# First chunk of a macaron block: affinities and choice in halves, and a new order of ScalarE's first work

## The reference

```python
def ffn(x, centroids, expert_biases, Ws_up, Ws_down, W_up, W_down):
    shared = silu(xf @ Ws_up) @ Ws_down
    aff = xf @ centroids.T                        # 64 experts
    _, idx = top_k(aff + expert_biases, 8)
    w = sigmoid(take_along_axis(aff, idx, axis=1))
    w = w / (sum(w, axis=-1, keepdims=True) + 1e-08)
    cw = zeros((T, E)).at[arange(T)[:, None], idx].add(w)
    h = silu(einsum('td,edf->etf', xf, W_up))     # F = 64
    y = einsum('etf,efd->etd', h, W_down)
    return shared + einsum('etd,te->td', y, cw)

def attn(x, Wq, Wk, Wv):
    q, k, v = x @ Wq.T, x @ Wk.T, x @ Wv.T
    return softmax(q @ k.T) / sqrt(128) @ v       # all 2048 keys

x = x + 0.5 * ffn(layernorm(x), ...)
x = x + attn(layernorm(x), Wq, Wk, Wv)
x = x + 0.5 * ffn(layernorm(x), ...)
```

## Time and profile before

| what | value |
|---|---|
| profiled execution, its own time | 541.02 us |
| its span, first to last instruction | 539.2 us |
| TensorE busy | 532.0 us (99%) |
| VectorE busy | 408.5 us (76%) |
| ScalarE busy | 407.0 us (75%) |
| GpSimd busy | 273.7 us (51%) |
| mean granted clock of TensorE | 1.000 |
| HBM traffic over the span | 133 GB/s |

### The profile page before, as it was taken

The page is one execution under the profiler, slowest core; times in us unless marked ns, Lnnn a source line. Parts: engine busy times, 40 slices in busy tenths (PEclk is TensorE's granted clock), DMA queues, the critical chain, the costliest instruction groups (busy, mean ns, idle before and its releaser), DMA issues.

```text
span 539.2 us, 8716 instructions
## 1 busy us (share of the span) xinstructions
PE 532.0 (99%) x2710; PEld 437.2 (81%) x2710; DVE 408.5 (76%) x933; ACT 407.0 (75%) x815; POOL 273.7 (51%) x242
## 2 busy tenths in 40 slices
PE   8999999999999999999999999999999999999997
PEld 6677887887888888799999999878887888788886
DVE  5998689877966677867777889779678767965664
ACT  6898778877877775866666657778779777877773
POOL 3689757775776764000000000267676676766663
PEclk9999999999999999999999999999999999999999
DMA  8675555554555550000000000155565565556662
GB/s 264 194 220 200 189 182 167 179 197 150 172 187 193 190 160 1 2 1 0 1 2 1 2 1 0 50 193 171 166 195 169 168 202 169 182 157 204 202 193 84
DMA packets 44270, 72.25 MB, mean 134 GB/s; under 512 B 8864, under 2 KB 9632, under 8 KB 44224
## 3 DMA queue, kind: packets, MB, share of 16 engines
q1 hardware_dynamic: 43568, 71.17, 42.0%
q10 hardware_dynamic: 592, 0.39, 0.3%
q0 software_dynamic: 64, 0.13, 0.1%
HBM read 69.57 MB, written 2.10 MB: 133 GB/s over the span
## 4 chain that ended last, share of the span: by engine, by line
PE 93%; DVE 3%; ACT 2%; issue 1%; POOL 0%; DVEq 0%; POOLq 0%
PE lrow L1174 13%; PE lrow L1175 13%; PE lrow L1176 13%; PE bank L1216 11%; PE bank L1218 10%; PE bank L1217 10%; PE bank L1279 5%; PE bank L1501 3%; PE bank L1503 3%; PE bank L1502 3%; PE bank L1393 1%; PE bank L1286 1%; PE bank L1175 1%; PE bank L1176 1%; PE bank L1174 1%
## 5 line engine op out<-in xcount | busy, mean ns | idle before, releaser
L295 POOL TENSOR_TENSOR gpart_lo<-gated,gpart_hi 128x512 fp32r<-128x512 f32 x174 | 223.7, 1295 | 162.9 <-ACT gpart_hi L462 161.3
L451 ACT ACTIVATE lrow<-lrow 128x512 f32<-128x512 f32 (+1 forms) x245 | 143.9, 587 | 62.4 <-PE lrow L1176 61.9
L718 DVE TENSOR_TENSOR gated<-lrow,wide 128x512 f32<-128x512 f32 x170 | 116.1, 683 | 56.3 <-ACT lrow L451 53.6
L462 ACT CAST gpart_hi<-gated 128x512 fp32r<-128x512 f32 x174 | 106.7, 613 | 5.9 <-DVE gated L718 5.3
L1216 PE MATMUL bank<-gpart_lo,wdn_hi 128*128 128x512 f32 x246 | 97.7, 397 | 0.0
L1218 PE MATMUL bank<-gpart_hi,wdn_hi 128*128 128x512 f32 x246 | 97.7, 397 | 0.0
L1217 PE MATMUL bank<-gpart_hi,wdn_lo 128*128 128x512 f32 x246 | 97.0, 394 | 0.0
L718 DVE TENSOR_TENSOR lrow<-lrow,wide 128x512 f32<-128x512 f32 x74 | 51.4, 695 | 26.9 <-ACT lrow L451 26.9
L1092 DVE TENSOR_TENSOR pT_lo<-bank,pT_hi 128x512 fp32r<-128x512 f32 x64 | 43.6, 683 | 21.7 <-ACT pT_hi L650 21.7
L295 DVE TENSOR_TENSOR gpart_lo<-lrow,gpart_hi 128x512 fp32r<-128x512 f32 (+1 forms) x83 | 56.5, 681 | 1.6 <-ACT gpart_hi L462 1.3
L650 ACT CAST pT_hi<-bank 128x512 fp32r<-128x512 f32 x64 | 38.1, 595 | 24.1 <-PE bank L1279 23.9
(11 more groups left out here) (281 smaller groups left out, 978.2 us busy)
## 6 DMA issues: line engine op xcount, KB each, us to landing
wide<-gates_dram SPq DMA_DIRECT2D x488, 128.0 KB, 3.0
raw<-in_w_up SPq DMA_DIRECT2D x8, 256.0 KB, 5.5
raw<-in_w_down SPq DMA_DIRECT2D x8, 256.0 KB, 5.7
gates_dram<-gates SPq DMA_DIRECT2D x8, 128.0 KB, 2.3
x<-in_x SPq DMA_DIRECT2D x3, 256.0 KB, 3.9
out_dram<-x SPq DMA_DIRECT2D x3, 256.0 KB, 3.1
x<-in_x SPq DMA_DIRECT2D x1, 128.0 KB, 2.3
x<-in_x ACTq DMA_DIRECT2D x1, 128.0 KB, 2.5
```

Source lines behind the costliest of these rows:

```text
L295: return eng.tensor_tensor(gpart[1][0:m, U % NGP, :], gated_at(U)[0:m, :], gpart[0][0:m, U % NGP, :].bitcast(F32), ALU.subtract)
L451: nc.scalar.activation(dst[0:m, :], hid[U % NH][0:m, :], ACT.Silu).then_inc(s_silu, 1)
L462: nc.scalar.copy(gpart[0][0:m, U % NGP, :], gated_at(U)[0:m, :]).then_inc(s_ghi, 1)
L718: nc.vector.tensor_tensor(gated_at(U), a, b, ALU.mult).then_inc(s_gated, 1)
```

## The change

Six edits, all for the first chunk. (1) The affinities of tiles 2 and 3 go to another PSUM bank than those of tiles 0 and 1, each half has its own semaphore, and VectorE adds the bias and takes the maxima half by half; the sigmoid is two activations too. (2) GpSimd makes the cast of the small weights and waits, before its second `piece_lo`, for the experts' weights. (3) ScalarE makes the selector and the copy of the shared down weights before the first piece, and the second piece before the sigmoids. (4) ScalarE copies the turned weights before the third piece; the copy of the gates, and the pieces from the fourth on, come behind later units. (5) The transfer of the value weights moves from ScalarE's queue, and those of the query and key weights from GpSimd's queue, to SyncE at unit 31. (6) The semaphore for the shared down weights is split from that of the value weights.

```diff
@@ SyncE, chunk loop
                     if n == 0 and u % 2 == 1 and FIRST + (u - NB) // 2 < 2 * WP:
                         load_piece(FIRST + (u - NB) // 2)
+                    if n == 0 and u == 31:
+                        sp.dma_start(raws[:, E + F:LOADED], wv_d).then_inc(s_value, 16)
+                        for i, src in enumerate((wq_d, wk_d)):
+                            sp.dma_start(raw_qk[:, i * D:(i + 1) * D], src).then_inc(s_qk, 16)
@@ GpSimd
-            for i, src in enumerate((wq_d, wk_d)):
-                nc.gpsimd.dma_start(raw_qk[:, i * D:(i + 1) * D], src).then_inc(s_qk, 16)
             ...
+            pool.wait_ge(s_small, 16 * 2)
+            nc.gpsimd.tensor_copy(small[0][:, 0:E + F], raws[:, 0:E + F]).then_inc(s_wh0, 1)
             ...
                     if n == 0:
-                        for k in range(PRE):
+                        piece_lo(0)
+                        pool.wait_ge(p_cw, 1)
+                        for k in range(1, PRE):
                             piece_lo(k)
@@ ScalarE
+            def first_sil(h):
+                act.wait_ge(f_bias, h + 1)
+                nc.scalar.activation(sil[:, h * GT:(h + 1) * GT, :].rearrange("p t e -> p (t e)"),
+                                     (bank[0], mp)[h][:, 0:GT * E], ACT.Sigmoid).then_inc((f_sil, p_sil)[h], 1)
-            act.dma_start(raws[:, E + F:LOADED], wv_d).then_inc(s_value, 16)
-            act.wait_ge(s_small, 16 * 2)
-            nc.scalar.copy(small[0][:, 0:E + F], raws[:, 0:E + F]).then_inc(s_wh, 1)
                             first_hi(0)
                             first_hi(1)
-                            piece_hi(0)
-                            act.wait_ge(s_value, 16 * 3)
-                            nc.scalar.copy(wsdn[0][:, :], rawd[:, :]).then_inc(s_wh, 1)
                             act.wait_ge(s_spread, 1)
                             make_sel()
-                            act.wait_ge(f_bias, 1)
-                            nc.scalar.activation(flat(sil), bank[0][:, 0:TPC * E], ACT.Sigmoid).then_inc(p_sil, 1)
+                            act.wait_ge(s_sdn, 16 * 2)
+                            nc.scalar.copy(wsdn[0][:, :], rawd[:, :]).then_inc(s_wh, 1)
+                            piece_hi(0)
+                            piece_hi(1)
+                            first_sil(0)
+                            first_sil(1)
                             nc.scalar.activation(eps[:, 3:4], eps[:, 0:1], ACT.Silu)
-                            piece_hi(1)
                             silu_unit(0, n)
                             silu_unit(1, n)
                             hi_unit(0, n)
                             silu_unit(2, n)
+                            act.wait_ge(p_cwT, 1)
+                            nc.scalar.copy(cwT[:, :], mp[:, :]).then_inc(p_cwr, 1)
                             piece_hi(2)
+                            silu_unit(3, n)
+                            hi_unit(1, n)
                             pro_cwT(n)
-                            silu_unit(3, n)
-                    for u in range(7 if n == NCH else min(c, 1), UNITS):
+                            hi_unit(2, n)
+                            silu_unit(4, n)
+                            piece_hi(PRE)
+                            hi_unit(3, n)
+                            piece_hi(PRE + 1)
+                            silu_unit(5, n)
+                            hi_unit(4, n)
+                            piece_hi(PRE + 2)
+                    for u in range((6, 7)[f] if c == 0 else 1, UNITS):
@@ VectorE, first_top
-                dve.wait_ge(p_aff, 1)
-                nc.vector.tensor_tensor(b[:, :, :], bank[0][:, 0:TPC * E].rearrange("p (t e) -> p t e", e=E),
-                                        bc(bias[:, :]), ALU.add).then_inc(f_bias, 1)
-                dve.wait_ge(f_bias, 1)
-                for i in range(TPC):
-                    ins = nc.vector.max(top[:, i, :], b[:, i, :])
+                for h in range(2):
+                    some = slice(h * GT, (h + 1) * GT)
+                    dve.wait_ge((f_aff, p_aff)[h], 1)
+                    nc.vector.tensor_tensor(b[:, some, :], (bank[0], mp)[h][:, 0:GT * E].rearrange("p (t e) -> p t e", e=E),
+                                            bias[:, :].unsqueeze(1).to_broadcast([P, GT, E]), ALU.add).then_inc(f_bias, 1)
+                    dve.wait_ge(f_bias, h + 1)
+                    for i in range(h * GT, (h + 1) * GT):
+                        ins = nc.vector.max(top[:, i, :], b[:, i, :])
                 ins.then_inc(p_max, 1)
@@ TensorE, first_aff
-                    ins = product(bank[0][:, i * E:(i + 1) * E], [a[:, 0, i * P:(i + 1) * P] for a in xnT[0]], cen)
-                ins.then_inc(p_aff, 1)
+                    at = i % GT * E
+                    ins = product((bank[0], mp)[i // GT][:, at:at + E], [a[:, 0, i * P:(i + 1) * P] for a in xnT[0]], cen)
+                    if i % GT == GT - 1:
+                        ins.then_inc((f_aff, p_aff)[i // GT], 1)
```

More of the change, by code:

```diff
@@ L157, in macaron_kernel @@
         s_x0b = sem("x_in0_second_half")
-        s_small, s_value, s_qk, s_bias = sem("small_in"), sem("value_in"), sem("qk_in"), sem("bias_in")
+        s_small, s_sdn, s_value, s_qk, s_bias = (
+            sem("small_in"), sem("shared_down_in"), sem("value_in"), sem("qk_in"), sem("bias_in"))
         s_eps, s_zero = sem("eps_made"), sem("cw_zeroed")
@@ L162, in macaron_kernel @@
         s_pad = sem("wsdn_pad_zeroed")
-        f_xT, f_hi, f_lo, f_bias = (sem("first_" + n) for n in ("xT", "hi", "lo", "biased"))
+        f_xT, f_hi, f_lo, f_aff, f_bias, f_sil = (sem("first_" + n) for n in ("xT", "hi", "lo", "aff", "biased", "sigmoid"))
         s_raw = [sem(f"raw_in{i}") for i in range(NR)]
@@ L168, in macaron_kernel @@
         s_id, s_spread = sem("ident_made"), sem("spread_made")
-        s_wh, s_wl = sem("small_hi_made"), sem("small_lo_made")
+        s_wh0, s_wh, s_wl = sem("first_small_hi_made"), sem("small_hi_made"), sem("small_lo_made")
         s_whi = sem("weight_piece_hi")
@@ L491, in pro_cwT @@
                 act.wait_ge(p_cwT, n + 1)
-                if n % NCH == 0:
+                if n == NCH:
                     nc.scalar.copy(cwT[:, :], mp[:, :]).then_inc(p_cwr, 1)
@@ L585, in _ @@
                             silu_unit(2, n)
+                            act.wait_ge(p_cwT, 1)
+                            nc.scalar.copy(cwT[:, :], mp[:, :]).then_inc(p_cwr, 1)
                             piece_hi(2)
+                            silu_unit(3, n)
+                            hi_unit(1, n)
                             pro_cwT(n)
-                            silu_unit(3, n)
-                    for u in range(7 if n == NCH else min(c, 1), UNITS):
+                            hi_unit(2, n)
[7 more added lines that the diff above has]
+                    for u in range((6, 7)[f] if c == 0 else 1, UNITS):
                         if c or u >= LEADS[f]:
                             silu_unit(u, n)
-                        if c or u > 1 - f:
-                            hi_unit(*before(u, n))
+                        hi_unit(*before(u, n))
                         if n == 0 and u % 2 == 0 and PRE + u // 2 < 2 * WP:
@@ L620, in _ @@
                         if n == 1 and u == 4:
+                            act.wait_ge(s_value, 16)
                             nc.scalar.copy(small[0][:, E + F:LOADED], raws[:, E + F:LOADED]).then_inc(s_wh, 1)
@@ L983, in small_lo @@
                             def small_lo(k, parts, whole, lo, hi):
[L984 removed]
+                                dve.wait_ge(s_wh if k else s_wh0, max(k, 1))
                                 nc.vector.tensor_tensor(parts[1][:, lo:hi], whole[:, lo:hi], parts[0][:, lo:hi].bitcast(F32),
```

5 lines of the change are left out of this document (2 added, 3 removed).

## The result

The changed kernel takes 542.42 us (median of 22 runs, 541.56 to 543.27), the kernel before 541.18 on the same chip (22 runs). The ratio is 1.0018, 95% interval 1.0012 to 1.0025: 1.0 us slower (0.6 to 1.4), less than the 0.5% that the prediction set as its bound for a change. The medians differ by 1.24. The ratio is smaller: it agrees with that of the means, 542.35 and 541.36, and one long execution, 543.68, lifts the mean of the kernel before (such executions are the subject of the last experiment). The profiled execution has a span of 540.5, 1.3 above the 539.2 of before. The forecast was 1.4 us slower, at 542.9.

The account below looks back on a forecast made before the run. TensorE's matmul stream and its holes bound the kernel (93% of the span). VectorE's wait for GpSimd's root (1.3) plus unit 13's gates (0.1) gave +1.4 on 541.5: 542.9 us, range 540.9 to 544.8; the 0.2 gained earlier did not count.

Parts of the forecast that it names:

- Start: Before the affinities: the first transpose stays at 5.96 and everything up to the affinity products keeps its place within 0.05 us.
- Halves: VectorE's bias and maxima by halves: choice multiply moves from 11.33 to about 10.89, 0.44 us sooner (bounds 0.3 and 0.52).
- First piece 0.93 later: ScalarE's first piece at 8.32 moves the first expert product to 10.58; TensorE is free at 13.56, net gain 0.2 us.
- GpSimd's wait costs 0: GpSimd's second subtraction waits for the experts' weights (13.1); only subtractions needed behind 20 us follow, so cost 0.
- The root: GpSimd's second-chunk root ends at 22.8; VectorE's normalisation moves from 21.55 to 22.83: 1.3 us lost (bounds 0 and 2.3).
- Unit 13's gates: Late gates' copy: unit 13's second half lands at 34.7, its user comes at 34.45; 0.1 us lost (bounds 0 and 0.5).
- Loads at unit 31 cost nothing: SyncE issues gates of units 31 to 33 1.8 us later; unit 31's, 0.8 late, covered by 7 us before down matmuls.
- Rival B: Faster: GpSimd's root ends before VectorE needs it at 21.4, gaining 0.44 and 0.2, to 540.9 us; chance 0.14.
- Rival C: No change: the stall is given back as later first-chunk holes shrink by 1.1 us; +0.3, 541.8 us; chance 0.17.
- Rival D: Much slower: late gates count, 1.3 plus 0.25 at unit 13 and 0.8 at unit 31; +2.4, 543.9 us; chance 0.14.
- sign of being wrong: Second chunk: the forecast is wrong if GpSimd's root ends before 21.5 or the transposes come before 25.2.
- the other case: Clock rival: TensorE runs at half rate for 4 us behind the new hole, 2 us more, 544.9 us; chance 0.03.

Follow-up runs that it names:

- the last experiment: The run also called cast only: kernel before, with just the cast of the small weights moved from ScalarE to GpSimd; 540.96 us, ratio 0.9993.
- cast only: Kernel before, with just the cast of the small weights moved from ScalarE to GpSimd; 540.96 us, ratio 0.9993 to the kernel before.
- loads only: Kernel before, with just the loads of the value, query and key weights moved to SyncE at unit 31; 541.13 us, ratio 0.9996.
- halves only: Kernel before, with just the affinities, bias, maxima and sigmoids in halves; 540.75 us, ratio 0.9989.
- piece first: The head only kernel, with the first weight piece again ahead of the selector and the shared weights' copy; 540.34 us, ratio 0.9984 to the kernel before.
- one warm-up fewer: The head only kernel, with one warm-up matmul instead of two ahead of the expert weights' transposes; 540.29 us, ratio 0.9984 to the kernel before.
- head only: The change, with ScalarE's order of third piece, turned weights, gates' copy and later pieces put back as before; 540.46 us, ratio 0.9982 to the kernel before.
- Root first: The change, with GpSimd's reciprocal root for the second chunk ahead of the fourth piece's low part; 542.30 us, ratio 1.0016 to the kernel before.
- both: The change, with GpSimd's root ahead of the fourth piece and the gates' copy directly behind the turned weights' copy; 540.51 us, ratio 0.9984.
- gates early: The change, with the gates' copy directly behind the copy of the turned weights; 541.63 us, ratio 1.0006 to the kernel before.
- tail only: Kernel before, with just ScalarE's new order: turned weights ahead of third piece, gates' copy and later pieces behind later units; 542.64 us, ratio 1.0029.

## Why the prediction was right

By its own steps, in order:

- **Start** (tokens' transposes stay at 5.96, all up to the affinities within 0.05). Nearly. The transposes came at 5.90 and the first affinity product at 7.49 for 7.64. ScalarE's first cast of turned tokens had not waited for TensorE but for ScalarE's own table load, which ends sooner now (6.53 for 6.67). That is worth 0.08 to 0.15 (cast only: first affinity product at 7.56). Executions scatter by as much: that product stood at 7.36 to 7.62 with the cast on GpSimd, and at 7.62 to 7.67 in before, loads only and halves only. (The transfer that left ScalarE's queue was its fourth, not its third.)
- **Halves** (0.44 for the choice). The multiply came 0.61 sooner in the change and 0.49 in halves only.
- **First piece 0.93 later, first expert product at 10.58, TensorE's queue full up to 13.56.** The mechanism was right: the queue and not the weights held the transposes, and piece first and one warm-up fewer each take that away. The size was off. The first piece came at 8.09, not 8.32, since ScalarE's queue came to that place at 7.16 for 7.44 (halves only, whose edits lie behind it, had it at 7.25, so most of this is scatter), and I moved the product by the piece's full delay, though by the earlier trace rows the low part had ended at 9.49 and the product started at 9.70: 0.21 of slack. So it came at 10.14 and the transposes at 13.21, not 13.56: the head gained 0.38 there and 0.24 at the copy (0.64 instead of 0.88 from transposes to copy), where I counted 0.2 in all.
- **GpSimd's wait costs 0.** It costs nothing, and without it the choice multiply would take 0.46 longer: it gains about 0.2 by the timelines. I had the queue behind it right and did not ask what the subtraction does to VectorE beside it.
- **The root.** I had 22.83 for VectorE's normalisation and +1.3. It was 22.36 and **+0.82**. The delay behind the copy of the turned weights was nearly as large as counted: from that copy to the second chunk's transposes it is 10.30 in before and in head only and 11.74 in the change, 1.44 more, and I had 1.50. VectorE's idle part of it was 1.15, not the 1.43 from 21.4 to 22.83, because VectorE itself came to that place 0.3 later behind the copy than in head only. What was mis-sized is the time at which the queue walk begins: the copy of the turned weights stood at 13.85, not 14.25.
- **Unit 13's gates.** I took 0.1 from bounds of 0 and 0.5. It was **0.43**: VectorE's wait of 0.82 for 0.25 expected. VectorE came earlier than counted, since the root did, while the transfers stood almost where I had them (34.6 for 34.7). The two terms aren't independent: whatever one bound gives back, the next takes. Root first shows the extreme of this, 1.28 given back at the root and 1.1 of it taken by gates. So 0.1 was the price of the gates behind a late root only; by themselves they cost 1.4 of span (root first against both), and the root by itself 1.0 (gates early against both).
- **Loads at unit 31 cost nothing.** Right, by loads only and by the change's own row. But the cover that I counted on was not needed: unit 31's gates were to land 0.8 late for VectorE, and they landed at 61.0, before their use at 61.39.
- **Sum.** 0.82 + 0.43 = 1.25, and 1.3 of span. Forecast 1.4. Two errors of 0.5 and 0.3 with opposite signs met, and that the sum came within 0.2 is luck to that extent; the mechanism, GpSimd's root and then unit 13's gates, is what the trace shows. The forecast of 542.9 stands 0.5 above the measured 542.42, mostly because I took 541.5 for the kernel before, from four times, where 22 gave 541.18. Neither sign of being wrong came: the root ended at 22.32, not before 21.5, and the transposes stood at 25.59, not before 25.2.

Rival B needed the root before 21.4; head only shows what it described, with a median 0.6 below before, as B priced it. Rival C, holes later in the first chunk that shrink, did not come: the holes behind 46 are the same. Rival D had the right mechanism for unit 13 and the wrong one for unit 31. The clock kept its upper level behind the new hole of 1.48 at 25.59 (steps of 0.23 there), as the prediction took it. The 4 us at half pace by which I priced the other case stand in no run; the one fall in the midst of work, in tail only, lasted 6.8.

## What to carry to other kernels

Where an edit delays work that several consumers hang on, list all bounds behind it in order of time: one repaired alone may give back almost nothing, and it then looks as if it had been harmless (here 0.2 and 0.6 of 1.6 us of span). Price each bound by itself as well as behind the others. When you shift a consumer by its producer's delay, first take off the slack between the producer's end and the consumer's start. And a small cast that waits for a transfer belongs on an engine that has nothing urgent queued behind it.

## What the runs showed of the hardware

- A landing 1.0 us later at the start cost 2.6: TensorE had 1.67 us without work, and from 0.9 us behind the end of that hole the granted clock was 0.50 for 6.8 us. A hole nearly as long, 1.48 us before 25.59 in the change, was followed by 1.00. In the first case only the warm-up matmuls of the first 5.5 us stood before the hole, in the second some 18 us of work. The Trainium skill, "TensorE: Matmul & The Clock Gate", Part 1, says that the array falls back after being idle; the first trace agrees, with the fall shortly behind the hole, and the second shows a hole where it did not.
- VectorE's multiply of two SBUF operands, 128 by 256, took 0.89 us beside a GpSimd subtraction and 0.43 without it, while its marking steps (0.195 from one to the next) did not slow beside the same subtraction. The Trainium skill, "SBUF — State Buffer", section "SBUF: two separate sides", says that VectorE with two SBUF inputs and GpSimd take turns for a whole instruction. The trace agrees roughly: had the multiply stood until the subtraction's end at 11.28 and then taken 0.43, it would have ended at 11.71; it ended at 11.56. The small step of halves only (128 by 48, 0.21 alone) ended at 13.19 behind a subtraction that ended at 13.13, also 0.15 sooner than by such a sum. A multiply of the same size as the first, but with one operand in PSUM (`cw<-rec,bank`), took 0.41 beside that subtraction, as it does without one.
- The same 32 KB transfer landed 2.5 to 4.3 us behind its issue in five executions with the same transfers at the start (before, tail only twice, halves only, cast only), and a 128 KB one of gates 3.3 to 5.0 within the kernel before.
